# Metaformer block with position-aware row attention and a sigmoid recurrence: projections and relative parts as four 32x32 matmuls, relative parts by image pairs, elementwise work dealt anew to ScalarE and GpSimd

## The chip, the cores and the metric

One core of one Trainium2 chip runs the kernel. The metric is the device time of one execution in microseconds; the time before is the median of three runs. All data is float32.

## The reference, cut to what matters

The input x has 16 images of 32 x 32 x 32 (channel, row, position). The block normalises over the last axis, attends, adds the input, normalises again, multiplies by a 32x32 matrix, normalises over the batch, and runs a recurrence.

```python
x = x + attention(layernorm(x, 1e-6))         # below
t = tokens(x); n = layernorm(t, 1e-5)
q, k, v = Wq @ y, Wk @ y, Wv @ y              # over channels, per (row i, position j)
qk  = sum_i q[n,c,i,j] * k[n,c,h,j] / d       # per position j: scores between rows i and h
qrq = sum_i q[n,c,i,j] * rq[c,h,i] / d        # relative parts, linear in y
krk = sum_i k[n,c,i,j] * rk[c,h,i] / d
w   = softmax(qk + Gq*qrq + Gk*krk, axis=3)
out = w . (Gv1*v)  +  w . (Gv2*rv)            # weighted sum, and relative values
wx  = n @ W.T ; wx = batchnorm(wx)*gamma + beta
y_t = sigmoid(wx_t + y_{t-1} @ V.T)           # 1024 steps per image in the token order
out = t + y
```

In the kernel q and k are never formed alone: u = (Wk.T Wq / d) y is projected, and the scores are u against y. The relative parts come from one factor r, made out of Wq, Wk, rq, rk and the gates, applied to y.

## The kernel before, in words

**Layout.** 128 partitions hold 4 groups (g) of 32 channels, that is 4 images; the free dimension holds 4 image quarters (q, "images" below), 32 rows and 32 positions, so that one q is 1024 columns. A half or unit is 16 rows (512 columns, one PSUM bank). Engines run in a hand-written order, and named semaphores tie them together.

**First normalisation** (lines 595 to 638 on VectorE, 341 to 346 on GpSimd, 414 to 441 on ScalarE). Per part: sum over the last axis (`ln_mean`), mean by a `tensor_scalar` (L601), centring (`ln_minus`, L158; on VectorE for the two halves of image 0, on GpSimd for images 1 to 3), square on ScalarE (L419), sum of squares (L608), variance by a `tensor_scalar` (L611), square root on ScalarE (L437), reciprocal (L617) and scaling (L164).

**Weights.** SyncE loads everything, in the order of lines 278 to 296. GpSimd clears the block-diagonal tiles `w_bd`, `m_bd`, `r_tile` and `rv_bd` (L328 to L347). ScalarE writes the 32x32 diagonal blocks of `m_bd` (L431), of `r_bd` (`set_r`, L402, four copies of 32 x 1024) and of `rv_bd` (`set_rv`, L411, four more). VectorE spreads the gates (L565), turns the weights (L582) and writes `w_bd` (L587, L589).

**Attention on TensorE** (lines 877 to 1063). `project_u(q)` (L901) is two 128x128 matmuls of 512 columns; `scores(q, jh)` (L912) is 16 positions x 4 groups of 32x32 matmuls; `relative_scores` (L953) is, for all four images at once, 32 matmuls of 128x128 against 128 columns, one for each row; `project_values` (L943) is one 128x128 matmul a unit; `relative_values` (L931) spreads rv; `value_rows(b)` (L994) is four 128x128 matmuls; `weighted_sums(q, jh)` (L981) is 64 matmuls of 32x32; `project_wx(k)` (L1010) is one 128x128 matmul. Each float32 matmul stands in the profile as two LDWEIGHTS and two MATMUL rows. `keep_warm` (L887) issues matmuls whose result is not used. Long and short work are interleaved: `scores(2, 0)`, two value projections, `scores(2, 1)`, and so on; `value_rows` stands between halves of `weighted_sums`.

**Softmax.** VectorE adds scores and relative part out of PSUM (L650) and takes the row maximum (L655); GpSimd subtracts it (L354); ScalarE takes exp (L461); VectorE sums (L659), inverts (L661) and multiplies (`weights`, L663). `turn_values` (L643) transposes the values, reading them with a stride. 

**Second normalisation and wx.** VectorE adds the relative values and the input (`add_relative`, L680), then the weighted sum (`residual`, L689), sum and mean (L694, L696), sum of squares and variance (L705, L708), reciprocal (L713), transpose (`t_turn`, L727) and the batch statistics (L732). GpSimd centres (L361) and scales (L367) units 0 to 6, ScalarE squares (L484), takes roots (L489) and copies wx out of PSUM (L494). The last unit is centred and scaled on VectorE (L699, L717). `bn_aggr` (L789) ends this stage.

**Recurrence** (L1084 on TensorE, L546 on ScalarE, L810 on VectorE) and the output (L317, L323, L302) follow.

## Time and profile before

| | |
|---|---|
| time of the kernel, median of 3 runs | 159.18 us (157.61 to 159.52) |
| span of the profiled execution | 157.0 us |
| the runs' time less that span | 0.6 to 2.5 us, 2.2 at the median |
| busy: TensorE matmul, VectorE, ScalarE, GpSimd | 116.0, 121.8, 66.5, 48.1 us |
| attention and normalisations, to the end of L789 | 0 to 126.0 us |
| recurrence and output | 126.0 to 157.0 us |

The span goes from the first to the last instruction of one execution; a run's time holds what lies around it as well. In the profile PE is TensorE's matmuls, PEld its weight loads, DVE VectorE, ACT ScalarE, POOL GpSimd and SP SyncE. In a timeline row stand start, duration, engine, line, operation, what is written and read, and the number of instructions that were merged; in brackets stands the idle time of the engine before it and what ended it, where "issue" means that nothing in the profile accounts for it.

### The profile page before, as it was taken

The numbers are of one execution on the slowest core, as the hardware profiler recorded it, in microseconds if no ns is written. First come the engines' busy times: TensorE is split into PE (matmuls) and PEld (weight loads), VectorE is DVE, ScalarE is ACT, GpSimd is POOL, SyncE is SP. The second block draws the span as 40 slices with busy tenths as digits, with TensorE's granted clock in tenths as the row PEclk, the third lists the DMA queues.
The fourth block names the chain that finished last, engine by engine and source line by source line (L and its number), as shares of the span: only waits on it lengthen the run. The fifth ranks groups of instructions, "written<-read, shape, count | busy, mean of one in ns | idle before, by whom it ended". The sixth has DMA issues, their size and how long they took to land.

```text
span 157.0 us, 5384 instructions
## 1 busy us (share of the span) xinstructions
PE 116.0 (74%) x2404; PEld 80.3 (51%) x2404; DVE 121.8 (78%) x190; ACT 66.5 (42%) x155; POOL 48.1 (31%) x48
## 2 busy tenths in 40 slices
PE   0856969049996999858889955995795679999500
PEld 0412364027995563843559955651541147999500
DVE  1988999984044919859894888979999959788993
ACT  3431665054662440951410052134313447999600
POOL 6911935900004403104000222754532000002950
PEclk9996895857999599755999996598699955999955
DMA  3692000000000000000000000000000000000467
GB/s 138 172 301 47 0 4 4 0 0 0 0 8 4 0 8 4 4 4 0 4 4 4 4 0 4 4 4 0 4 0 2 0 4 2 0 0 0 138 183 218
DMA packets 6611, 5.02 MB, mean 32 GB/s; under 512 B 1756, under 2 KB 5852, under 8 KB 6588
## 3 DMA queue, kind: packets, MB, share of 16 engines
q1 hardware_dynamic: 6588, 4.67, 10.5%
q8 instruction: 19, 0.31, 0.8%
q14 instruction: 4, 0.03, 0.1%
HBM read 2.58 MB, written 2.10 MB: 30 GB/s over the span
## 4 chain that ended last, share of the span: by engine, by line
DVE 43%; PE 31%; ACT 14%; issue 6%; POOL 2%; DMA 2%; ACTq 0%
PE ps L912 8%; ACT warm L546 5%; PE ps L953 5%; DVE stat L611 4%; PE ps L901 4%; PE ps L943 4%; DVE xin L317 3%; DVE stat L694 3%; DVE stat L599 3%; DVE x L689 3%; DVE stat L601 3%; DVE stat L705 3%; DVE u_tile L727 3%; DVE y L323 3%; PE ps L994 3%
## 5 line engine op out<-in xcount | busy, mean ns | idle before, releaser
L981 PE MATMUL ps<-att,yt_tile 32*32 32x32 f32 x1024 | 16.6, 229 | 5.6 <-issue 3.9
L901 PE MATMUL ps<-y,m_bd 128*128 128x512 f32 x16 | 13.6, 1000 | 9.3 <-ACT u_tile L395 6.1
L981 PEld LDWEIGHTS ps<-att,yt_tile 32*32 32x32 f32 x1024 | 15.3, 129 | 9.5 <-issue 8.5
L912 PEld LDWEIGHTS ps<-y,u_tile 32*32 32x32 f32 x1024 | 15.6, 145 | 8.5 <-issue 8.4
L912 PE MATMUL ps<-y,u_tile 32*32 32x32 f32 x1024 | 16.7, 228 | 4.1 <-issue 4.1
L354 POOL TENSOR_TENSOR att<-att,soft 128x1024 f32<-128x1024 f32 x4 | 7.7, 1916 | 33.6 <-DVE soft L655 33.6
L650 DVE TENSOR_TENSOR att<-ps,bias_tile 128x1024 f32<-128x1024 f32 x4 | 4.9, 1224 | 16.0 <-ACT bias_tile L451 8.1
L484 ACT ACTIVATE square<-x2n 128x512 f32<-128x512 f32 x8 | 5.0, 628 | 24.9 <-POOL x2n L361 24.4
L887 PE MATMUL ps<-xin 128*128 128x512 f32 x22 | 14.8, 824 | 0.0
L323 POOL TENSOR_TENSOR y<-xin,x 128x256 f32<-128x256 f32 (+1 forms) x7 | 7.1, 1046 | 24.7 <-DVE xin L317 24.7
L1010 PE MATMUL ps<-u_tile,w_bd 128*128 128x512 f32 x16 | 10.5, 751 | 4.8 <-DVE u_tile L727 4.2
L361 POOL TENSOR_TENSOR x2n<-x,stat 128x512 f32<-128x512 f32 x7 | 7.3, 1048 | 21.8 <-DVE stat L696 21.7
L810 DVE TENSOR_SCALAR ps<-bias_tile,bnv 128x512 f32<-128x512 f32 (+1 forms) x18 | 12.4, 762 | 1.9 <-ACT warm L546 1.8
L901 PEld LDWEIGHTS ps<-y,m_bd 128*128 128x128 f32 x16 | 4.3, 299 | 15.4 <-issue 15.3
L367 POOL TENSOR_TENSOR x2n<-x2n,stat 128x512 f32<-128x512 f32 x7 | 7.3, 1048 | 11.0 <-DVE stat L713 11.0
L1084 PEld LDWEIGHTS ps<-warm,w_bd 128*128 128x128 f32 x80 | 10.0, 205 | 1.0 <-DVE ps L810 0.5
L1084 PE MATMUL ps<-warm,w_bd 128*128 128x128 f32 x80 | 9.9, 289 | 0.0
L943 PE MATMUL ps<-y,w_bd 128*128 128x512 f32 x16 | 9.4, 716 | 0.0
L887 PEld LDWEIGHTS ps<-xin 128*128 128x128 f32 x22 | 5.5, 267 | 6.8 <-issue 5.8
L546 ACT ACTIVATE warm<-ps 128x128 f32<-128x128 f32 x40 | 8.9, 276 | 0.2
L456 ACT COPY r_tile<-ps 128x512 f32<-128x512 f32 x8 | 4.7, 584 | 9.0 <-PE ps L943 9.0
L994 PE MATMUL ps<-att,rv_bd 128*128 128x128 f32 x64 | 7.9, 280 | 0.7 <-DVE att L663 0.7
(97 smaller groups left out, 227.2 us busy)
## 6 DMA issues: line engine op xcount, KB each, us to landing
out_dram<-y SPq DMA_DIRECT2D x8, 256.0 KB, 2.4
xin<-in_x_dram SPq DMA_DIRECT2D x3, 512.0 KB, 6.3
xin<-in_x_dram SPq DMA_DIRECT2D x2, 256.0 KB, 2.8
r_in<-in_L_conv_rq_dram SPq DMA_DIRECT2D x1, 128.0 KB, 4.8
r_in<-in_L_conv_rk_dram SPq DMA_DIRECT2D x1, 128.0 KB, 5.7
rv_in<-in_L_conv_rv_dram SPq DMA_DIRECT2D x1, 128.0 KB, 7.4
gates<-in_L_conv_Gv_dram SPq DMA_DIRECT2D x2, 0.5 KB, 4.9
wsmall<-in_L_conv_Wk_dram SPq DMA_DIRECT2D x1, 16.0 KB
```

Source lines behind the costliest of these rows:

```text
L323: return eng.tensor_tensor(result[:, :, rows, :], back[:, at:at + P * k].rearrange("p (q i j) -> p q i j", q=Q, i=k), x2[:, :, rows, :], A ...
L546: nc.scalar.activation(state_out(t, r), rec_slot(t, r).rearrange("p (q c) -> p q c", q=Q), ACT.Sigmoid).then_inc(S["state"], 1)
L810: return nc.vector.tensor_scalar(out, rows, scl, shift, ALU.mult, ALU.add)
L887: ins = nc.tensor.matmul(bank(k), xin[:, 0, 0:4, :].rearrange("p i j -> p (i j)"), xin[:, 0, 0:16, :].rearrange("p i j -> p (i j)"), start ...
L901: nc.tensor.matmul(bank(k), m_bd[:, :], y[:, q, 16 * k:16 * (k + 1), :].rearrange("p i j -> p (i j)"), start=True, stop=True).then_inc(S[" ...
L912: ins = nc.tensor.matmul(ps[p, half_scores(q, j // 16), C * (j % 16):C * (j % 16 + 1)], u[p, q, :, j], y[p, q, :, j], start=True, stop=True)
L943: nc.tensor.matmul(bank(k % 2), w_bd[:, 0, :], unit(y, k).rearrange("p i j -> p (i j)"), start=True, stop=True).then_inc(S["value_product" ...
L953: ins = nc.tensor.matmul(bank(6 + b % 2)[:, P * k:P * (k + 1)], r_bd[:, ROWS * b + k, :], y[:, :, ROWS * b + k, :], start=True, stop=True)
L981: ins = nc.tensor.matmul(ps[p, WSUM_BANK[q] + jh, C * (j % 16):C * (j % 16 + 1)], v_t[p, q, j, :], att[p, q, :, j], start=True, stop=True)
L994: ins = nc.tensor.matmul(rows[:, :, k, :], rv_bd[:, ROWS * b + k, :], att[:, :, ROWS * b + k, :], start=(k == 0), stop=True, skip_group_ch ...
L1010: nc.tensor.matmul(bank(WX_BANK[k % 2]), w_bd[:, 1, :], tokens[:, 16 * (k % 2):16 * (k % 2 + 1), k // 2, :], start=True, stop=True).then_i ...
L1084: nc.tensor.matmul(rec_slot(t, r), w_bd[:, 2, :], state_in(t, r), start=False, stop=True, skip_group_check=True).then_inc(S["preact"], 1)
```

## The change

- `m_bd`, `r_bd`, `rv_bd` and the value part of `w_bd` go. `m_fac`, `r_fac`, `rv_t` and `wv` hold the factor once for each group of 32 partitions, and each 128x128 matmul that used them becomes four 32x32 matmuls, one a group. `w_bd` keeps two block-diagonal matrices (W and V).
- The relative scores and the relative values are made for two images at a time, in four parts of eight rows, each row being four matmuls of 32x32 against 64 columns.
- ScalarE copies the relative values out of PSUM into `x2`, and GpSimd adds the input (`add_input`); VectorE's `add_relative` goes. GpSimd multiplies by the softmax's reciprocal (`weigh`) and centres all parts of the first normalisation; it also writes `w_bd`.
- The variance's scale and epsilon go into ScalarE's square root. The means are made by `scalar_tensor_tensor` with a tile of zeros in place of `tensor_scalar`.
- ScalarE issues six of the DMAs (Wk, Wq, rq, rk, Gq, Gk), SyncE issues all of x first, rv is loaded four times, and ScalarE spreads the gates. `preload_act_table(ACT.Sqrt)` stands ahead of ScalarE's work.
- `values` is stored position-major, so that its transposition reads contiguously. TensorE's order is coarser.

```diff
-            for k in range(2):
-                    nc.tensor.matmul(bank(k), m_bd[:, :], y[:, q, 16 * k:16 * (k + 1), :].rearrange("p i j -> p (i j)"),
-                                     start=True, stop=True).then_inc(S["u_product"], 1)
+                for k in range(2):
+                    for g in range(G):
+                        p = group(g)
+                        ins = nc.tensor.matmul(bank(k)[p, :], m_fac[p, :],
+                                               y[p, q, 16 * k:16 * (k + 1), :].rearrange("p i j -> p (i j)"),
+                                               start=True, stop=True)
+                    ins.then_inc(S["u_product"], 1)
...
+            def eight_rows(n, by, of, done):
+                pair, part = n // PARTS, n % PARTS
+                for k in range(EIGHT):
+                    i = EIGHT * part + k
+                    for g in range(G):
+                        p = group(g)
+                        ins = nc.tensor.matmul(eight_bank(n)[p, 2 * C * k:2 * C * (k + 1)].rearrange("p (q j) -> p q j", q=2),
+                                               by[p, i, :], of[p, 2 * pair:2 * pair + 2, i, :], start=True, stop=True)
+                ins.then_inc(S[done], 1)
...
+            pe.wait_ge(S["x_in0"], 16)
+            keep_warm(2, 2)
+            relative_factor()
+            pe.wait_ge(S["m_set"], 1)
+            project_u(0)
+            scores(0)
+            project_u(1)
+            relative_scores(0)
+            scores(1)
+            project_u(2)
+            project_u(3)
+            relative_scores(1)
+            scores(2)
+            project_values(0)
+            project_values(1)
+            scores(3)
+            project_values(2)
+            project_values(3)
+            weighted_sums(0)
+            relative_values(0)
+            weighted_sums(1)
+            pe.wait_ge(S["x2_ready"], 2)
+            for n in (4, 5, 6, 7):
+                project_values(n)
+            weighted_sums(2)
+            project_wx(0)
+            project_wx(1)
+            relative_values(1)
+            project_wx(2)
+            weighted_sums(3)
+            project_wx(3)
...
+            mark_bank(6)
+            mark_bank(7)
+            mark_bank(0)
+            mark_bank(1)
+            project_wx(4)
+            mark_bank(4)
+            mark_bank(5)
+            project_wx(5)
+            project_wx(6)
+            project_wx(7)
```

VectorE's and GpSimd's new pieces, and VectorE's order:

```diff
+                nc.vector.scalar_tensor_tensor(out=stat[:, 1, q, rows], in0=stat[:, 0, q, rows], scalar=1.0 / C,
+                                               in1=nought[:, 0:k], op0=ALU.mult, op1=ALU.add).then_inc(S["ln_mean"], 1)
...
+            def add_input(n):
+                pool.wait_ge(S["relv_ready"], n + 1)
+                nc.gpsimd.tensor_tensor(eight(x2, n), eight(x2, n), eight(xin, n), ALU.add).then_inc(S["x2_part"], 1)
...
+            score_max(0)
+            score_max(1)
+            weight_sum(0)
+            dve.wait_ge(S["rv_scaled"], 1)
+            nc.vector.transpose(rv_t[:, :, :], rv_s[:, :, :]).then_inc(S["rv_set"], 1)
+            weight_sum(1)
+            score_max(2)
+            score_max(3)
+            weight_sum(2)
+            turn_values(0)
+            turn_values(1)
+            weight_sum(3)
...
+            residual(4)
+            residual(5)
+            bn_part(2)
+            bn_part(3)
+            t_sum2(4)
+            t_rstd(4)
+            t_sum2(5)
             t_rstd(5)
             t_turn(4)
-            bn_part(3)
             residual(6)
             residual(7)
+            t_turn(5)
+            t_sum2(6)
             t_rstd(6)
+            t_sum2(7)
+            bn_part(4)
             t_turn(6)
             t_rstd(7)
             t_turn(7)
```

ScalarE's start:

```diff
+            load_small(3, Wk, "wqk_in")
+            load_small(4, Wq, "wqk_in")
+            for k, a in enumerate((rq, rk)):
+                act.dma_start(r_in[group(k), :], a.rearrange("c h i -> c (h i)")).then_inc(S["r_in_s"], 16)
+            load_gate(0, Gq, "gates_in")
+            load_gate(1, Gk, "gates_in")
+            nc.scalar.preload_act_table(ACT.Sqrt)
...
+            spread_out(0, 4)
+            spread_out(1, 3)
+            act.wait_ge(S["m_product"], 1)
+            nc.scalar.mul(m_fac[:, :], ps[:, 1, 0:C], 1.0 / d).then_inc(S["m_set"], 1)
+            ln_square(0)
+            ln_square(1)
```

## Rows read from the trace of the kernel before

**Rows 1.** The page's part 1: busy us (share of the span) xinstructions.
```profile
PE 116.0 (74%) x2404; PEld 80.3 (51%) x2404; DVE 121.8 (78%) x190; ACT 66.5 (42%) x155; POOL 48.1 (31%) x48
```
**Rows 2.** Timeline of TensorE's matmuls through the dense 32x32 work.
```profile
18.77 3.05 PE L912 MATMUL ps<-y,u_tile 32*32 32x32 f32 x200
23.16 1.03 PE L912 MATMUL ps<-y,u_tile 32*32 32x32 f32 x56 [1.34 <-issue]
...
44.54 3.84 PE L912 MATMUL ps<-y,u_tile 32*32 32x32 f32 x255
49.67 0.25 PE L912 MATMUL ps<-y,u_tile 32*32 32x32 f32 x1 [1.29 <-issue]
...
62.66 3.61 PE L912 MATMUL ps<-y,u_tile 32*32 32x32 f32 x234
67.73 0.51 PE L912 MATMUL ps<-y,u_tile 32*32 32x32 f32 x19 [1.47 <-issue]
...
71.28 0.54 PE L981 MATMUL ps<-att,yt_tile 32*32 32x32 f32 x23 [1.51 <-issue]
...
110.49 2.02 PE L981 MATMUL ps<-att,yt_tile 32*32 32x32 f32 x128
```
**Rows 3.** Waits, whole span: us in total, times, longest.
```profile
PE ps L912 <- issue: 4.1, 3, 1.5
PE ps L981 <- issue: 3.9, 3, 1.7
```
**Rows 4.** The page's part 3, the queue that brings instructions.
```profile
q8 instruction: 19, 0.31, 0.8%
```
**Rows 5.** Timeline, matmuls of 512 columns against 128x128 weights.
```profile
54.62 1.98 PE L943 MATMUL ps<-y,w_bd 128*128 128x512 f32 x4
...
71.75 4.28 PE L943 MATMUL ps<-y,w_bd 128*128 128x512 f32 x6
```
**Rows 6.** Windows: length, PE, PEld, DVE, ACT, POOL busy (x), PEclk, DMA share, GB/s.
```profile
52.70:53.70 1.00, 1.00 (x73) 1.00 (x76) 0.97 (x2) 0.59 (x1) 1.00 (x1) 0.50 0.00 0
108.87:125.99 17.12, 12.28 (x148) 5.06 (x147) 16.09 (x34) 5.48 (x13) 5.24 (x5) 0.90 0.01 1
```
**Rows 7.** Timeline and the page's part 6: when y of image 0 is ready; a gate's DMA.
```profile
12.46 0.69 DVE L164 TENSOR_TENSOR y<-y,stat 128x512 f32<-128x512 f32 x1
...
gates<-in_L_conv_Gv_dram SPq DMA_DIRECT2D x2, 0.5 KB, 4.9
```
**Rows 8.** Groups by line, shapes apart, whole span: busy us, mean ns of one.
```profile
L663 DVE TENSOR_TENSOR att<-att,soft 128x1024 f32<-128x1024 f32 x4 | 5.2, 1302 | 0.1
L680 DVE TENSOR_TENSOR x<-ps,xin 128x512 f32<-128x512 f32 x8 | 5.1, 675 | 2.3 <-PE ps L994 2.3
L643 DVE STREAM_TRANSPOSE yt_tile<-r_tile 128x1024 f32<-128x1024 f32 x4 | 7.8, 1950 | 0.5 <-ACT r_tile L456 0.5
L727 DVE STREAM_TRANSPOSE u_tile<-x2n 128x512 f32<-128x512 f32 x8 | 5.3, 687 | 0.0
L655 DVE TENSOR_REDUCE soft<-att 128x32 f32<-128x1024 f32 x4 | 4.9, 1220 | 0.1
L354 POOL TENSOR_TENSOR att<-att,soft 128x1024 f32<-128x1024 f32 x4 | 7.7, 1916 | 33.6 <-DVE soft L655 33.6
L361 POOL TENSOR_TENSOR x2n<-x,stat 128x512 f32<-128x512 f32 x7 | 7.3, 1048 | 21.8 <-DVE stat L696 21.7
L456 ACT COPY r_tile<-ps 128x512 f32<-128x512 f32 x8 | 4.7, 584 | 9.0 <-PE ps L943 9.0
L411 ACT COPY rv_bd<-ps 32x1024 f32<-32x1024 f32 x4 | 4.0, 1006 | 5.6 <-PE ps L931 5.5
```
**Rows 9.** Timeline: VectorE's operations that met GpSimd's.
```profile
26.22 5.34 DVE L611 TENSOR_SCALAR stat<-stat 128x32 f32<-128x32 f32 x1
...
52.52 1.92 POOL L354 TENSOR_TENSOR att<-att,soft 128x1024 f32<-128x1024 f32 x1 [2.71 <-DVE soft L655]
...
53.98 1.53 DVE L663 TENSOR_TENSOR att<-att,soft 128x1024 f32<-128x1024 f32 x1
```

More of the change, by code:

```diff
@@ L177, in wx_rows, with eight, eight_bank, ln_scale @@
             return wx_q[:, 16 * (k % 2):16 * (k % 2 + 1), k // 2, :]
+        def eight(t, n):
+            pair, part = n // PARTS, n % PARTS
+            return t[:, 2 * pair:2 * pair + 2, EIGHT * part:EIGHT * (part + 1), :]
+        def eight_bank(n):
+            return bank(REL_BANK[n % 2])
+        def ln_scale(eng, n, done):
+            q, row, k = LN_PARTS[n]
+            eng.tensor_tensor(y[:, q, row:row + k, :], y[:, q, row:row + k, :],
+                              stat[:, 3, q, row:row + k].unsqueeze(2).broadcast_to([P, k, C]),
+                              ALU.mult).then_inc(S[done], 1)
         def round_row(t):
@@ new lines, in _ @@
+            u_half(2, 0)
+            u_half(2, 1)
+            u_half(3, 0)
+            u_half(3, 1)
+            score_exp(1)
+            for n in range(PARTS, 2 * PARTS):
+                rel_out(n)
+            score_exp(2)
+            value_out(0)
+            value_out(1)
+            value_out(2)
+            value_out(3)
+            score_exp(3)
+            relv_out(0)
+            relv_out(1)
+            relv_out(2)
+            relv_out(3)
+            for n in (4, 5, 6, 7):
+                value_out(n)
@@ new lines, in _ @@
+            ln_mean(1)
+            ln_mean(2)
+            ln_sum2(0)
+            ln_sum2(1)
+            ln_rstd(0)
+            ln_out(0)
+            ln_rstd(1)
+            ln_out(1)
+            ln_mean(3)
+            ln_sum2(2)
+            ln_rstd(2)
+            ln_out(2)
+            ln_mean(4)
+            dve.wait_ge(S["w_in"], 16 * 3)
+            nc.vector.transpose(wturned[:, :, :], wsmall[:, 0:3, :]).then_inc(S["turned"], 1)
+            ln_sum2(3)
+            ln_rstd(3)
+            ln_sum2(4)
@@ L778, in _ @@
             t_turn(7)
-            bn_part(4)
             dve.wait_ge(S["marked"], 2)
@@ L959, in _ @@
-            project_u(0)
-            relative_factor()
-            scores(0, 0)
-            scores(0, 1)
-            project_u(1)
-            project_u(2)
-            wait_y(pe, Q - 1)
-            relative_scores()
-            def weighted_sums(q, jh):
+                for jh in range(2):
+                    for j in range(16 * jh, 16 * (jh + 1)):
+                        for g in range(G):
+                            p = group(g)
+                            ins = nc.tensor.matmul(ps[p, SCORE_BANK[q] + jh, C * (j % 16):C * (j % 16 + 1)],
+                                                   u[p, q, :, j], y[p, q, :, j], start=True, stop=True)
+                    ins.then_inc(S["score_product"], 1)
@@ L970, in weighted_sums, with relative_values @@
+            def relative_values(pair):
+                pe.wait_ge(S["weights"], 2 * pair + 2)
+                pe.wait_ge(S["rv_set"], 1)
+                pe.wait_ge(S["rel_ready"], 2 * PARTS)
+                for n in range(PARTS * pair, PARTS * (pair + 1)):
+                    if n >= 2:
+                        pe.wait_ge(S["relv_ready"], n - 1)
+                    eight_rows(n, rv_t, att, "relv_product")
+            def weighted_sums(q):
                 pe.wait_ge(S["weights"], q + 1)
@@ L998, in mark_bank @@
-            def mark_bank(k):
-                pe.wait_ge(S["x2_ready"], UNITS - 2 if k >= 6 else UNITS)
-                keep_warm(k, 1).then_inc(S["marked"], 1)
+                    pe.wait_ge(S["score_sum"], 4)
+                for jh in range(2):
+                    for j in range(16 * jh, 16 * (jh + 1)):
+                        for g in range(G):
+                            p = group(g)
+                            ins = nc.tensor.matmul(ps[p, WSUM_BANK[q] + jh, C * (j % 16):C * (j % 16 + 1)],
+                                                   v_t[p, q, j, :], att[p, q, :, j], start=True, stop=True)
+                    ins.then_inc(S["wsum_product"], 1)
```

602 lines of the change are left out of this document (250 added, 352 removed).

## The prediction

> **What bounds the kernel now.** I read the page's busy shares first, then TensorE's timeline, its waits, the DMA queues, and last the windows and the groups by line. The busy shares name two engines: VectorE 121.8 us and TensorE 116.0 us of 157.0 [rows 1]. Most of the edit takes work from VectorE, so the question is what TensorE allows once VectorE is quicker.
>
> In TensorE's timeline the reader is to see holes inside runs of 32x32 matmuls. `scores(0)` does 200 MATMUL rows in 3.05 us, stands still for 1.34 us and does the other 56; more holes of 1.29, 1.47 and 1.51 us follow [rows 2]. The waits put six such holes, 8.0 us, down to "issue": no engine released them [rows 3]. From the first hole to the second lie 56 + 8 (L901) + 64 (L953) + 255 = 383 MATMUL rows, or three times 128; from the third to the fourth about 127. 
>
> The Trainium skill, "Runtime: NRT & Kernel Launch", section "Instruction fetch mechanics", also has 16 KiB blocks of 256 instructions, but says that crossing one is mostly hidden. The size agrees with rows 3 and 4, the "mostly hidden" does not. By the page there would be no growing cost here; that is the first rival.
>
> **The change, part by part.**
>
> *TensorE's instruction count.* Relative scores and relative values go from 64 MATMUL rows each to 2 pairs x 4 parts x 8 rows x 4 groups x 2 = 512 each; the projections of u and of values from 16 each to 64 each. That is +992, from 2404 to about 3390: nearly eight more packets, all in the stage that ends at 126.0.
>
> *What a projection costs.* Four 32x32 matmuls of 512 columns do as much as the block diagonal if they run side by side, and save nothing. A pair of full-width matmuls took 0.99 us (1.98 for two halves) and 1.43 (4.28 for three) [rows 5]; I take 1.15 for a half. Do four groups run side by side? With the granted clock at 0.50 (1.2 GHz) 73 MATMUL rows of 32 columns started in 1 us [rows 6], 14 ns each. 512 columns take at least the 0.71 us of rows 5's slower row (4.28 / 6) at that clock, so 32 columns take 45 ns or more: 45/14 says that over three are under way at once, of four that could be. Bounds for 512 columns: 0.99 us a half, and, if a group's second pass held up the next group's first, five passes instead of two, 2.5 to 3.6 us. I take side by side, as rows 6 stand nearest.
>
> *What VectorE loses.* `weights` 5.2 us, `add_relative` 5.1 us, four strided transpositions of 1.95 us that read contiguously now (between 1.95 and 2 x 0.69 = 1.37; I take 1.37) [rows 8], the variances, and the stalls of `tensor_scalar` behind GpSimd, of which one lasted 5.34 us [rows 9]. ScalarE loses eight block copies of 1.0 us and gains eight of 0.58; GpSimd gains four of 1.92 and eight of 1.05 [rows 8]. Both have room [rows 1], but their steps now lie in chains.
>
> *The `scalar_tensor_tensor`.* It reads two tiles of SBUF. A two-tile operation meeting GpSimd's subtraction took 1.53 us against a mean of 1.30 [rows 9, 8]; GpSimd's ended at 54.44, and 1.22 us of work after 54.3 is just what VectorE shows. So the mean can still wait, up to 1.9 us, and only the long train is avoided. I charge 0.8 us near the end and nothing ahead of it, where TensorE's packets cover it. The Trainium skill, "SBUF — State Buffer", section "Who interferes with whom", says the same against this edit: a VectorE instruction with two SBUF inputs contends with a GpSimd instruction that reads SBUF.
>
> **The sum,** along TensorE:
>
> 1. Start. ScalarE now issues six DMAs and waits for the gates ahead of its first square. A gate's DMA took 4.9 us to land [rows 7]; issued sixth, near 3.3 us, it lands near 8 by that row, and between 6 and 11 if half or one and a half times that is allowed. I take 8, so y of image 0 is ready near 12.6 us (before: 12.46 + 0.69 = 13.15 [rows 7]), and since the relative factor is already made, `scores(0)` starts at 16.0 instead of 18.77 [rows 2].
> 2. To the end of `scores(3)`: 4 x 256 score rows and 2 x 256 relative rows are 12 packets, 12 x 3.4 = 40.8. Eight projection halves add 9.2. They hide about 3.5 holes of 1.45, 5.1. End: 60.9. Before it was 67.73 + 0.51 = 68.24 [rows 2]. The change leads by 7.3 us.
> 3. `weighted_sums(0)` needs the turned values, which in VectorE's order stand behind the sum and maximum of image 3 and the sum of image 2: 3 x 1.22 + 0.35 + 1.37 = 5.4. Start: 66.3, before 68.0. Lead 1.7.
> 4. To the end of `weighted_sums(3)`: 4 x 256 + 2 x 256 rows, again 40.8; seven halves (four values, three of wx) 8.0; 4.5 holes hidden, -6.5; 2.5 for hand-offs from ScalarE and GpSimd, an estimate. End 111.1, before 110.49 + 2.02 = 112.5 [rows 2]. Lead 1.4.
> 5. The tail. In the 17.1 us after `residual(5)` VectorE was busy for 16.1 [rows 6]. The change keeps that list, less one `bn_part` that went ahead (0.7) and four variances (1.5 with their stalls): 14.9. But `residual(5)` is later against TensorE (last relative part, ScalarE's copy, GpSimd's addition), and `bn_part(3)` waits for `project_wx(3)`, now behind all of `weighted_sums(3)`: 1.15 + 0.6 + 0.1 after it. So 14.2 us of list remain from there, with 2 us of waits inside and the 0.8 above: 111.1 + 1.9 + 14.2 + 2.8 = 130.0, before 126.0.
>
> The recurrence and the output are untouched. That is +4.0 on the profiled execution: 161 us of span, and with the 2.2 us that lie around it at the median, 163.2. I put the time at **163 us**. VectorE becomes the idler engine, and TensorE pays for it in packets.
>
> **The rivals.**
>
> *A: the holes stay hidden; faster.* If a packet is ready as soon as it is needed, steps 2 and 4 lose eight and a half and seven and a half holes of 1.45, 23 us, of which VectorE's own order gives back about 6: 163 - 17 = 146. For it: VectorE has some 20 us less to do, and all six holes lie in dense runs, none where 32x32 work is mixed with 128-wide work. Against it: the change mixes less, and its runs are longer. With the holes at 1.0 us instead of 1.45 the time is 163 - 16 x 0.45 = 156, which is where faster by over 2% begins.
>
> *B: the four groups run one after another at 512 columns.* Sixteen halves at 2.5 us or more instead of 1.15 are +22 to +27, of which hidden holes give some back: about 183. The rule that speaks for it: the Trainium skill, "TensorE: Matmul & The Clock Gate", Part 3, has matmuls start and end in program order, and each group's two passes stand side by side in that order. Against it are the 14 ns of rows 6.
>
> *C: no difference.* The same chain with a packet ready after 3.2 us instead of 3.4 and half of the tail's waits: 24 x 0.2 + 1 = -6 at most, halved by what overlaps: 159 to 160.
>
> *D: the edit doesn't do what it says.* The `scalar_tensor_tensor` stalls as the `tensor_scalar` did, thirteen times, a few on the path: +3, 166. And if the sparse 32x32 work lowers the granted clock to 1.2 GHz for most of the stage, fifteen halves cost 0.5 more: +5, 168. These lie inside the forecast's upper end.
>
> **How the numbers follow.** Forecast with D: 0.50, slower by over 2% but for its lowest part. C 0.27, A 0.18, B 0.05. Two per cent, 3.2 us, is about what a measurement tells from no change. Faster by over 2%: 0.18; within: 0.28; slower: 0.54. The range reaches down to A with two thirds of a hole (153) and up to D with a late gate and a second slow term (174); beyond lie the whole of A and B.
>
> **What would show it.** Right: the instruction queue shows 26 or 27 packets; TensorE's idle time by "issue" grows from 8 to 20 us and more; `scores(3)` ends near 61, `weighted_sums(3)` near 111, `bn_aggr` near 130; VectorE is busy for under 100 us; a projection half of four groups lasts 1 to 1.4 us. Wrong: "issue" stays under 12 us and `weighted_sums(3)` ends before 100 (A); halves of 2.5 us (B); or the holes are as told, but another engine is late at each of them.

## The result, and the profile after

The changed kernel takes 182.5 us (180.54 to 185.12, 4 runs) against 158.84 us (157.61 to 159.52, 4 runs) beside it: a ratio of 1.146, 95% interval 1.137 to 1.154. It is slower by 23.7 us. (Medians are of all runs, and ratios of those alone that lie within 1.5% of their kernel's fastest, so 182.5 / 158.84 isn't exactly 1.146.) Forecast were 163, with 174 as the upper end. The direction was right, and the size was far off.

The profile's page of the changed kernel, parts 1 and 3, answers to [rows 1] and [rows 4]:

```profile
span 180.1 us, 7348 instructions
PE 120.9 (67%) x3390; PEld 79.4 (44%) x3390; DVE 93.1 (52%) x152; ACT 65.8 (37%) x156; POOL 61.3 (34%) x66
q8 instruction: 26, 0.43, 1.0%
```

VectorE lost 28.7 us of work, and the instructions come in 26 packets instead of 19, both as forecast. No engine is busier than TensorE's 67%. The waits of the changed kernel (total, times, longest) answer to [rows 3]:

```profile
PE ps L969 <- issue: 10.6, 7, 1.9
PE ps L908 <- issue: 9.4, 6, 2.0
PE ps L918 <- issue: 4.0, 5, 1.7
```

In these 18 holes TensorE stands still for 24.0 us with no engine to name for it; before it was 8.0 us in six. The timeline of its matmuls, against [rows 2]:

```profile
17.55 1.92 PE L895 MATMUL ps<-y,m_fac 32*32 32x512 f32 x16 [0.95 <-DVE y L156]
20.17 2.93 PE L908 MATMUL ps<-y,u_tile 32*32 32x32 f32 x190 [0.70 <-ACT u_tile L437]
24.18 1.14 PE L908 MATMUL ps<-y,u_tile 32*32 32x32 f32 x65 [1.09 <-issue]
...
36.18 2.03 PE L908 MATMUL ps<-y,u_tile 32*32 32x32 f32 x128 [2.01 <-issue]
39.91 1.41 PE L908 MATMUL ps<-y,u_tile 32*32 32x32 f32 x82 [1.70 <-issue]
...
67.36 0.33 PE L908 MATMUL ps<-y,u_tile 32*32 32x32 f32 x7 [1.25 <-issue]
67.49 3.63 PE L940 MATMUL ps<-y,wv 32*32 32x512 f32 x16
72.94 1.69 PE L969 MATMUL ps<-att,yt_tile 32*32 32x32 f32 x104 [1.81 <-DVE yt_tile L653]
76.55 2.02 PE L969 MATMUL ps<-att,yt_tile 32*32 32x32 f32 x128 [1.93 <-issue]
80.28 0.55 PE L969 MATMUL ps<-att,yt_tile 32*32 32x32 f32 x24 [1.71 <-issue]
...
95.74 7.10 PE L940 MATMUL ps<-y,wv 32*32 32x512 f32 x32
...
126.86 1.19 PE L969 MATMUL ps<-att,yt_tile 32*32 32x32 f32 x69 [1.73 <-issue]
```

In the dense stretches the merged counts show the packets themselves: runs of exactly 128 matmuls, a hole, then the rest. From the start of one such run to the start after the next hole is 3.73 us (36.18 to 39.91, and 76.55 to 80.28). Line by line against before:

| event | before | after | forecast |
|---|---|---|---|
| scores(0) starts | 18.77 | 20.17 | 16.0 |
| scores(3) ends | 68.24 | 67.7 | 60.9 |
| weighted_sums(0) starts | 68.0 | 72.94 | 66.3 |
| weighted_sums(3) ends | 112.5 | 128.05 | 111.1 |
| bn_aggr ends | 126.0 | 149.2 | 130.0 |

What lies behind bn_aggr is the same in both (31.0 and 30.9 us). So the miss of 19.2 us has four parts: 4.2 at the start, 2.6 in the first dense phase, 10.3 in the second, 2.2 in the tail, less 0.2 between the phases.

### The profile page after: what moved, and what is told of

Read it like the earlier page. It is cut to its first block, busy times and chain, and to the rows that moved or that the text cites. A ratio compares the mean times of both kernels' runs of the same rounds, so it can differ in the third digit from the quotient of the medians.

```text
span 180.1 us, 7348 instructions
## 1 busy us (share of the span) xinstructions
PE 120.9 (67%) x3390; PEld 79.4 (44%) x3390; DVE 93.1 (52%) x152; ACT 65.8 (37%) x156; POOL 61.3 (34%) x66
## 4 chain that ended last, share of the span: by engine, by line
PE 44%; DVE 21%; issue 16%; ACT 11%; DMA 5%; ACTq 2%
PE ps L908 9%; PE ps L918 8%; PE ps L969 7%; PE ps L895 6%; PE ps L940 6%; PE ps L980 5%; DMA gates<-in_L_conv_Gk_dram 5%; ACT warm L585 4%; DVE xin L286 3%; DVE y L292 2%; PE ps L875 2%; DVE stat L706 2%; DVE u_tile L724 2%; ACT yt_tile L585 2%; DVE stat L694 2%
## 5 line engine op out<-in xcount | busy, mean ns | idle before, releaser
L969 PE MATMUL ps<-att,yt_tile 32*32 32x32 f32 x1024 | 16.8, 229 | 13.2 <-issue 10.6
L689 DVE TENSOR_TENSOR x<-ps,x 128x512 f32<-128x512 f32 x8 | 5.4, 675 | 20.6 <-POOL x L356 20.6
L940 PE MATMUL ps<-y,wv 32*32 32x512 f32 x64 | 14.5, 1032 | 0.0
L356 POOL TENSOR_TENSOR x<-x,xin 128x512 f32<-128x512 f32 x8 | 10.0, 1265 | 13.1 <-ACT x L457 13.1
L309 POOL TENSOR_TENSOR y<-xin,stat 128x1024 f32<-128x1024 f32 (+1 forms) x5 | 7.8, 1566 | 15.2 <-DVE stat L610 15.2
L918 PE MATMUL ps<-att,rv_t 32*32 32x64 f32 x512 | 10.5, 247 | 3.3 <-issue 3.3
L918 PEld LDWEIGHTS ps<-att,rv_t 32*32 32x32 f32 x512 | 9.7, 128 | 5.2 <-issue 5.2
L895 PE MATMUL ps<-y,m_fac 32*32 32x512 f32 x64 | 11.3, 843 | 0.9 <-DVE y L156 0.9
L616 DVE TENSOR_REDUCE stat<-square 128x32 f32<-128x1024 f32 (+1 forms) x5 | 4.9, 994 | 11.4 <-ACT square L418 11.4
L452 ACT COPY values<-ps 128x512 f32<-128x512 f32 x8 | 4.6, 584 | 17.0 <-PE ps L940 17.0
L530 ACT COPY bias_tile<-ps 128x512 f32<-128x512 f32 x8 | 4.6, 584 | 15.9 <-PE ps L980 15.9
```

Source lines behind the costliest of these rows:

```text
L309: nc.gpsimd.tensor_tensor(y[:, q, row:row + k, :], xin[:, q, row:row + k, :], stat[:, 1, q, row:row + k].unsqueeze(2).broadcast_to([P, k, C]),
L356: nc.gpsimd.tensor_tensor(eight(x2, n), eight(x2, n), eight(xin, n), ALU.add).then_inc(S["x2_part"], 1)
L895: ins = nc.tensor.matmul(bank(k)[p, :], m_fac[p, :], y[p, q, 16 * k:16 * (k + 1), :].rearrange("p i j -> p (i j)"), start=True, stop=True)
L918: ins = nc.tensor.matmul(eight_bank(n)[p, 2 * C * k:2 * C * (k + 1)].rearrange("p (q j) -> p q j", q=2), by[p, i, :], of[p, 2 * pair:2 * p ...
L940: ins = nc.tensor.matmul(bank(k)[p, :].rearrange("p (j h) -> p j h", h=C), wv[p, :], y[p, q, :, 16 * k:16 * (k + 1)].rearrange("p h j -> p ...
L969: ins = nc.tensor.matmul(ps[p, WSUM_BANK[q] + jh, C * (j % 16):C * (j % 16 + 1)], v_t[p, q, j, :], att[p, q, :, j], start=True, stop=True)
```

## The experiments

Fourteen kernels ran; they are told in four groups. Their edits are shown shortened, with plain names for slices of tiles. Names that begin with a_ are the changed kernel with an edit, with b_ the kernel before with one. The kernel before took 158.4 to 159.1 us beside them (medians).

**1. Are the holes packets of instructions? (a_long, b_twice)**

a_long: the relative parts as one long matmul for each group and part. It applies one row's factor to all eight rows of a part, so it leaves the true relative parts out; it has 896 MATMUL rows fewer.

```diff
-for k in range(EIGHT):
-    for g in range(G):
-        matmul(eight_bank(n)[p, 2*C*k:2*C*(k+1)], by[p, i, :], of[p, 2*pair:2*pair+2, i, :])
+for g in range(G):
+    matmul(eight_bank(n)[p, :], by[p, EIGHT*part, :], of[p, 2*pair:2*pair+2, EIGHT*part:EIGHT*(part+1), :])
```

> The changed kernel with each part of the relative scores and values made by one matmul of 512 columns a group instead of eight rows of 64 columns. The columns that pass through the array, the banks and all waits stay; the MATMUL rows go from 1024 to 128 in the two relative products. It leaves out seven of eight row factors, so it computes other relative parts. Theory (instruction packets of 128 matmul pairs, 3.4 to 3.9 us each in dense work): 7 packets fewer, 19 instead of 26; the 16 parts cost some 1.2 us each instead of half a packet of 3.8; the time falls from 182.5 by 14 to 22 us, to 161 to 168. Rival (the array's work and the order bound TensorE, not the fetching): 16 parts stay near 1.0 to 1.2 us each, the time stays within 3 us of 182.5.

Measured: 165.74 us (163.42 to 168.06, 2 runs), 19 packets. Its waits:

```profile
PE ps L969 <- issue: 5.1, 4, 1.7
PE ps L908 <- issue: 3.5, 4, 1.2
```

b_twice: the kernel before, with scores(1) issued twice, so that the matmuls of image 1 are done again with the same result.

```diff
-ins = nc.tensor.matmul(...)
+for _ in range(2 if q == 1 else 1):
+    ins = nc.tensor.matmul(...)
```

> The kernel before with each matmul of scores(1) issued twice, the same operands and the same result: 256 more MATMUL rows, two packets. Theory (packets): scores(1) costs two more packets at 3.4 to 3.9 us less what was hidden, +6 to +8 us: 165 to 167, and 21 packets. Rival (issue at 15 ns a pair alone): +3.8 us: 163.

Measured: 167.4 us, ratio 1.061 (1.048 to 1.074), 21 packets. The timeline of TensorE where the work was doubled:

```profile
50.92 2.13 PE L913 MATMUL ps<-y,u_tile 32*32 32x32 f32 x128 [1.24 <-issue]
54.37 2.15 PE L913 MATMUL ps<-y,u_tile 32*32 32x32 f32 x128 [1.32 <-issue]
57.83 0.27 PE L913 MATMUL ps<-y,u_tile 32*32 32x32 f32 x1 [1.30 <-issue]
```

256 more matmuls of 15 to 17 ns are about 4 us of work and cost 8.5. One hole stands after every 128, in this dense stretch; the rival's 3.8 falls. And 896 matmuls taken out of the changed kernel give 16.8 us back, with the same columns through the array; its holes fell from 24.0 to 8.6 us.

The traces also say when each packet comes. The DMA view of b_twice from 52 to 53 us (forty slices of 0.025 us; a transfer is put in the slice in which it starts, and the share is of 16 engines):

```profile
DMA  9000000000000000000000000000000000000000
q8 instruction: 1, 0.02, 6.0%
```

and that of the changed kernel from 37 to 38 us:

```profile
DMA  0000000000090000000000000000000000000000
q8 instruction: 1, 0.02, 8.0%
```

In b_twice the packet starts at 52.0, 1.1 us after the run of 128 at 50.92 began; its transfer takes 0.96 us (6.0% of 16 us), and the next run begins at 54.37, 1.4 us after it landed. That makes the 3.45 us from run to run. In the changed kernel it starts at 37.3, 1.1 us after 36.18, takes 1.28 us, and the run at 39.91 begins 1.3 us after it landed: 3.73 us, longer by the slower transfer. Read in the same way, each of the changed kernel's 18 holes ends 1.2 to 1.5 us after an instruction packet has landed. In both cases, then, the next packet is fetched only once TensorE is inside the one before it, and work that is shorter than this round leaves a hole. Why the fetch doesn't start earlier no run here shows.

**2. Do four 32x32 matmuls of 512 columns run side by side? (b_four)**

```diff
-nc.tensor.matmul(bank(k), m_bd[:, :], y[:, q, 16*k:16*(k+1), :])
+for g in range(G):
+    ins = nc.tensor.matmul(bank(k)[p, :], m_bd[p, p], y[p, q, 16*k:16*(k+1), :])
```

> The kernel before with the projections of u and of the values as four 32x32 matmuls of 512 columns each, nothing else changed (the factors are read out of the diagonal blocks). Theory (the four groups run side by side; what counts is the instruction count): 96 more MATMUL rows, under one packet: 0 to +3 us, halves of 1.0 to 1.8 us as before. Rival (the groups run one after another): halves of 2.5 us or more and +15 to +25 us.

Measured: 158.72 us (10 runs), ratio 1.004 (0.998 to 1.010). Its timeline:

```profile
53.94 0.60 PE L949 MATMUL ps<-y,w_bd 32*32 32x512 f32 x1
...
54.04 1.90 PE L949 MATMUL ps<-y,w_bd 32*32 32x512 f32 x15
```

Sixteen MATMUL rows (two halves, four groups, two passes each) take 2.0 us, as the full-width pairs do in [rows 5]. Side by side is shown, and the forecast's rival B falls, although its 183 is the number that came out: right by accident, for a reason that isn't there. The changed kernel's own row at 17.55 says the same, 0.96 us a half. The rule quoted for B (matmuls start and end in program order) doesn't keep four row and column groups apart.

**3. The parts that could explain the miss (a_loads, a_values, b_contig, a_inter, a_mix, a_mix_long)**

a_loads: the six loads of ScalarE's queue go back to SyncE's, in the order of before.

```diff
+load_small(3, Wk) load_small(4, Wq) load_gate(0, Gq) load_gate(1, Gk)   # SyncE, after load_x(1)
+sp.dma_start(r_in ...) x2                                               # SyncE, after load_x(2)
-load_small(3, Wk) load_small(4, Wq) act.dma_start(r_in ...) x2 load_gate(0, Gq) load_gate(1, Gk)   # ScalarE
```

> The changed kernel with all loads back on SyncE's queue, the small ones between the halves of x and its rest, as before the change. Theory (the start is late because the gates and Wk, Wq wait behind 2 MB of x): scores(0) starts near 16 us instead of 20.2, and since TensorE is fetch-bound behind it, all of 3 to 5 us comes through to the end: 178 to 180. Rival (VectorE's and GpSimd's order sets the start or makes up for it): under 1.5 us of gain.

Measured: 178.12 us, ratio 1.129 (1.117 to 1.142): 4.4 us better. The intervals of the two ratios overlap a little, but the slowest of its five runs (178.73) is below the fastest of the changed kernel (180.54). ScalarE's timeline, the changed kernel first:

```profile
12.62 0.83 ACT L431 ACTIVATE spread<-wsmall,gates 32x128 f32<-32x128 f32 x2 [6.43 <-DMA gates<-in_L_conv_Gk_dram]
```

and the same instruction in a_loads:

```profile
6.31 0.83 ACT L434 ACTIVATE spread<-wsmall,gates 32x128 f32<-32x128 f32 x2 [4.29 <-DMA gates<-in_L_conv_Gk_dram]
```

A gate of a few bytes, issued near 4 us on a queue of its own, landed at 12.6, while issued on SyncE ahead of image 1 it was there at 6.3. scores(0) starts at 17.8 in a_loads instead of 20.2. Queue and order changed together here, so which of the two counts isn't separated.

b_contig: in the kernel before, value projections that read y with a stride of 32 elements, so that the transposition reads contiguously.

```diff
-matmul(bank(k % 2), w_bd[:, 0, :], unit(y, k))
+matmul(bank(k % 2) as (j h), w_bd[:, 0, :], y[:, k // 2, :, 16*(k % 2):16*(k % 2 + 1)] as (j h))
-transpose(v_t[:, q], values[:, q] as (j h))
+transpose(v_t[:, q], values[:, q])
```

> The kernel before with the values stored position-major, so that the value projection reads y with a stride and the transposition on VectorE reads contiguously. Theory: the transpositions take 1.2 us instead of 1.95 and two or three of them lie on the chain ahead of the weighted sums: -1 to -2.5 us. Rival (VectorE isn't what TensorE waits for there, the packets are): within 1 us of before; or the strided read slows the projections: slower.

Measured: 162.09 us, ratio 1.026 (1.018 to 1.034). Its timeline and a window on it:

```profile
55.80 3.69 PE L943 MATMUL ps<-y,w_bd 128*128 128x512 f32 x4
```

```profile
55.80:59.40 3.60, 3.60 (x9) 0.71 (x4) 1.63 (x2) 1.64 (x2) 0.59 (x1) 1.00 0.03 7
```

The transposition fell from 1.95 to 1.24 us. But four MATMUL rows take 3.69 us at the full granted clock, where [rows 5] has 1.98 for the same four: a moving operand with a stride of 128 bytes costs 0.92 us for 512 columns instead of 0.50. I had charged nothing for it. The expectation's last rival, a slower projection, holds.

a_values undoes just that in the changed kernel.

> The changed kernel with its values kept channel-major again, as before the change: the four 32x32 matmuls of a value half read 512 neighbouring columns instead of a stride of 32 elements, and VectorE's transposition reads with the stride (1.95 us instead of 1.22, four of them). The number of TensorE's instructions stays. Theory (the strided moving operand is one of the terms missing from the sum): the 64 matmuls of L940 fall from a mean of 1032 ns to about 600 ns, a half from 1.72 us to about 1.0 to 1.2, the eight halves together by 4 to 5 us, of which the four ahead of weighted_sums(0) are partly covered; transpositions give 0.7 back twice on the path: time 180 +- 1. Rival (the value projections cover packets that arrive anyway, so they cost nothing): 182.5 or up to 1.5 more, and idle time by 'issue' grows by what the projections lose.

Measured: 182.8 us (181.49 to 185.56, 4 runs): no difference from 182.5. The mean of L940 fell from 1032 to 830 ns:

```profile
62.62 3.64 PE L940 MATMUL ps<-y,wv 32*32 32x512 f32 x14
...
72.29 1.92 PE L940 MATMUL ps<-y,wv 32*32 32x512 f32 x16
78.41 1.70 PE L969 MATMUL ps<-att,yt_tile 32*32 32x32 f32 x104 [4.21 <-DVE yt_tile L653]
...
100.67 5.48 PE L940 MATMUL ps<-y,wv 32*32 32x512 f32 x32
```

The gain is there in places. The two halves ahead of weighted_sums(0) fell from 3.63 to 1.92 us, but the wait for VectorE behind them grew from 1.81 to 4.21; the four later halves fell from 7.10 to 5.48, and the whole phase from 55.1 to 53.1. The two halves at 62.62 did not change at all (3.64, as the two from 58.54 to 61.97 in the changed kernel, of which the windows are shown further down): in both, the granted clock stood at 0.50 there, which is 1.2 GHz. At that level the strided read costs nothing beside it; at 2.4 GHz it takes the gain of the clock away. My expectation of 180 missed, and the rival's number (182.5 to 184) holds, though not for its reason: idle time by "issue" stayed at 23.9 us. The eight halves gave up 3 to 4 us of TensorE's time, and the longer wait for VectorE and a later start took it. (The profiled execution was the slowest of the four, 185.56 us, and its gates landed late, so I compare its phases and not its end.)

a_inter deals the long matmuls between halves of scores(1) to (3) and weighted_sums(1), to hide more holes.

```diff
-scores(1); project_u(2); project_u(3)
+scores(1, (0,)); project_u(2); scores(1, (1,)); project_u(3)
-scores(2); project_values(0); project_values(1); scores(3); project_values(2); project_values(3)
+scores(2, (0,)); project_values(0); project_values(1); scores(2, (1,)); scores(3, (0,)); project_values(2); project_values(3); scores(3, (1,))
-weighted_sums(1); project_values(4); project_values(5)
+weighted_sums(1, (0,)); project_values(4); project_values(5); weighted_sums(1, (1,))
```

> The changed kernel with its long matmuls dealt between the halves of scores and of weighted_sums(1): project_u(2) and (3) between and behind the halves of scores(1), project_values(0) to (3) between the halves of scores(2) and (3), project_values(4), (5) between the halves of weighted_sums(1). Same instructions, another order on TensorE. Packet theory: each long matmul group among 32x32 work hides up to 1 to 1.9 us of a hole; three or four more holes are hidden, idle time by 'issue' falls from 24 to 19 us and the time to 176 to 180. Rival (a packet's arrival sets the pace and long work already hides all it can): 182.5 +- 1.5.

Measured: 180.06 us (177.63 to 181.98), ratio 1.126 (1.113 to 1.139), against 1.146 for the changed kernel. The intervals touch and the runs overlap, so a gain of some 2 us is likely and not shown. Of its 20.5 us of "issue", 5.2 are one wait of the kind told under a_mix.

a_mix has a_loads, a_values and a_inter together.

> The changed kernel with three repairs together: all loads on SyncE in the order of before (178.1 alone), values channel-major again, long matmuls dealt between halves. If the three are terms of one sum along TensorE: 178 minus 2 minus 3 to 4, that is 172 to 174. If they hide the same holes and give back one another's gain: 176 to 178. Either way it stays well above the kernel before, since TensorE still has 26 packets instead of 19: under 163 would speak against the packets as the main term.

Measured: 176.42 us (175.31 to 177.21), ratio 1.110 (1.100 to 1.119). One by one the three gave 4.4, -0.3 and 2.4 us, 6.5 in all; together they gave 6.1. Within the spread of the runs they add up. The expectation's second case has the right number, but what fell short of 172 to 174 is the size of the parts and not their sum. TensorE's timeline, then VectorE's:

```profile
75.82 3.50 PE L972 MATMUL ps<-att,yt_tile 32*32 32x32 f32 x231 [5.93 <-issue]
```

```profile
69.96 1.22 DVE L661 TENSOR_TENSOR att<-ps,bias_tile 128x1024 f32<-128x1024 f32 x1 [9.20 <-PE ps L911]
71.21 1.22 DVE L666 TENSOR_REDUCE soft<-att 128x32 f32<-128x1024 f32 x1
72.35 1.21 DVE L670 TENSOR_REDUCE soft<-att 128x32 f32<-128x1024 f32 x1
73.59 0.35 DVE L672 RECIPROCAL soft<-soft 128x32 f32<-128x32 f32 x1
73.86 3.65 DVE L656 STREAM_TRANSPOSE yt_tile<-values 128x1024 f32<-128x1024 f32 x2
```

The bracket says "issue" for 5.93 us, but this is no packet: the last one landed 4.8 us before the run began. It is the chain of step 3 on VectorE: sum, maximum, sum, reciprocal, and the first of two transpositions (73.86 + 1.9) ends 0.06 us ahead of weighted_sums(0). When project_values(2) and (3) moved ahead of the second half of scores(3), nothing was left to cover the chain. A label of a wait has to be held against the other engines' timelines before it is added up: of a_mix's 24.2 us of "issue", 18.3 are holes.

a_mix_long is a_mix with a_long's relative parts, so it too leaves the true relative parts out.

> The changed kernel with the loads in the order of before, values channel-major, long matmuls dealt between halves (176.4 with these), and the relative parts by one 32x32 matmul of 512 columns for each group and part, which multiplies all eight rows of a part by one row's factor (so other relative parts are computed, with 896 fewer MATMUL rows). Theory of packets: back to 19 packets, 16 to 18 less than 176.4: 158 to 161; with the fold of the variances still in it, it should even come under the kernel before (158.7) if nothing else were lost. Rival (the repairs and the packets hide one another): 163 to 166, as the relative parts alone gave 165.7.

Measured: 164.81 us, ratio 1.042 (1.024 to 1.059). That is a_long's 165.74 again, within its spread: once 896 matmuls are gone, the three repairs are worth nothing that shows. scores(0) starts 2.4 us earlier than in a_long (17.86 against 20.26), but weighted_sums(0) starts 1.8 us later (67.39 against 65.58), after 5.96 us of idle time for VectorE's chain, as above. The rival's number holds; that this wait alone decides the end is argued and not shown.

**4. What the good parts are worth (b_fold, b_fold_stt, b_pool, b_fsp, a_unfold)**

b_fold: the kernel before, with the variance folded into ScalarE's square root.

```diff
-nc.vector.tensor_scalar(var, sum2, 1.0 / C, EPS, ALU.mult, ALU.add)
-nc.scalar.activation(std, var, ACT.Sqrt)
+nc.scalar.activation(std, sum2, ACT.Sqrt, bias=eps, scale=1.0 / C)
```

> The kernel before with one part of the change alone: the variances' scale and epsilon go into ScalarE's square root, so VectorE's thirteen small tensor_scalar operations of the variances go, the 5.34 us one among them. Theory (that part of the change is good where TensorE isn't the bound): y of image 3 is ready 4 to 5 us earlier, TensorE's 6.1 us idle ahead of project_u(2) shrinks, and each t chain loses 0.2 us: 153 to 156. Rival (other waits take its place, since the image 2 scaling and two memsets still run on GpSimd): within 1 us of before.

Measured: 149.5 us, ratio 0.942 (0.933 to 0.950), more than expected. y of image 3 is ready at 27.7 us instead of 33.5: the variance of [rows 9] that took 5.34 us from 26.22 ended with GpSimd's memsets of `rv_bd` and `warm` (27.04 to 31.53), and it is gone. TensorE's 6.14 us of idle time ahead of project_u(2), which ended at 33.61, is gone too, and weighted_sums(3) ends at 102.94 instead of 112.5.

b_fold_stt: also the means by scalar_tensor_tensor with a tile of zeros.

> As the kernel with the variances folded into the square root, and the means by scalar_tensor_tensor with a tile of zeros, as the change has them. Theory (two inputs from SBUF wait for GpSimd only where it reads): the mean behind the r_tile memset loses its 2.3 us stall, the means behind GpSimd's centring keep theirs: 1 to 2.5 us less than with the fold alone. Rival (it stalls just as tensor_scalar does): no difference, or +0.5 us from its longer duration.

Measured: 147.71 us (144.93 to 149.04), bn_aggr ends at 114.9 where b_fold has 116.3. The runs of the two versions overlap by a little (b_fold 148.80 to 153.24), so this step rests on the rows more than on the medians. The groups by line, b_fold first:

```profile
L608 DVE TENSOR_SCALAR stat<-stat 128x16 f32<-128x16 f32 x2 | 3.4, 1704 | 0.1
L608 DVE TENSOR_SCALAR stat<-stat 128x32 f32<-128x32 f32 x3 | 1.9, 642 | 0.1
```

and b_fold_stt:

```profile
L611 DVE SCALAR_TENSOR_TENSOR stat<-stat,nought 128x16 f32<-128x16 f32 x2 | 0.4, 214 | 0.1
L611 DVE SCALAR_TENSOR_TENSOR stat<-stat,nought 128x32 f32<-128x32 f32 x3 | 1.9, 650 | 0.1
```

One of the two of 16 elements meets GpSimd's 3.51 us memset of `r_tile`, which reads nothing. Its row in the timeline of b_fold, and then in that of b_fold_stt:

```profile
5.70 3.14 DVE L608 TENSOR_SCALAR stat<-stat 128x16 f32<-128x16 f32 x1
```

```profile
5.74 0.17 DVE L611 SCALAR_TENSOR_TENSOR stat<-stat,nought 128x16 f32<-128x16 f32 x1
```

The three of 32 elements stand beside GpSimd's subtractions, which read SBUF: 642 and 650 ns, no difference. The Trainium skill, "SBUF — State Buffer", section "Who interferes with whom", has a VectorE instruction with two SBUF inputs contend with a GpSimd instruction that reads SBUF, and not with one that only writes it; the trace agrees with both halves. The stall behind the memset of `rv_bd` only moved on, in both versions: 3.50 us of VectorE's `spread_v`, a tensor_scalar, stand there now.

b_pool: the multiplication by softmax's reciprocal goes to GpSimd.

```diff
-nc.vector.tensor_tensor(att[:, q], att[:, q], soft_recip, ALU.mult)
+nc.gpsimd.tensor_tensor(att[:, q], att[:, q], soft_recip, ALU.mult)   # one image later in GpSimd's order
```

> The kernel before with the multiplication by the softmax's reciprocal on GpSimd, behind its subtraction for the next image, as in the change. Theory (moving work off VectorE is worth nothing where its step is in a chain): the multiplication takes 1.9 instead of 1.25 us and waits for its turn, VectorE gains 5 us of room: -1 to +2 us. Rival (VectorE's busy time is what counts): -3 to -5 us.

Measured: 159.21 us, ratio 1.002 (0.997 to 1.007). Five us of VectorE's work gone, and the time stays.

b_fsp is b_fold_stt with b_pool's edit.

> The kernel before with the variance folded into ScalarE's square root, the means by scalar_tensor_tensor (these two together gave 147.7) and, new, the multiplication by softmax's reciprocal on GpSimd, where it alone gave nothing. VectorE loses 5 us of work, the instruction count of TensorE stays 19 packets. Theory (with the head start of TensorE gone, VectorE's list of sums, maxima and transpositions behind scores(3) is late again): 145 to 147. Rival (the time between is set by TensorE's packets, as before): 147.7 +- 1.

Measured: 147.58 us (145.29 to 147.92). The same as b_fold_stt; VectorE's load doesn't bound that version either.

a_unfold: the changed kernel with its variances and means as tensor_scalars again.

> The changed kernel with one part of the edit undone: the variances are thirteen tensor_scalars on VectorE again (in place) and the means are tensor_scalars again. TensorE's program is the changed kernel's. In the kernel before, the same two edits were worth 11 us (158.4 to 147.7). Theory (the changed kernel had that gain, and the packets and the cold clock took about 35 us, not 23): undoing it costs 8 to 12, time 191 to 195. Rival (in the changed kernel TensorE's packets set the pace, so the gain never showed): 182.5 to 185, with scores(0) later by what the start loses and scores(3), weighted_sums(3) at the same times as before.

Measured: 185.98 us (181.93 to 186.67, 4 runs). Three of the four lie near 186 and one at 181.93, inside the changed kernel's own range (180.54 to 185.12), so no loss is shown; the medians differ by 3.5 us at most. The theory's 8 to 12 falls. In its profiled execution (185.97) scores(0) starts 1.3 us later, but 0.9 of that is a later landing of the gates (13.52 against 12.62), which the edit doesn't touch.

The rival's number fits, its reason isn't needed. The groups of the variances by line, in the kernel before and in a_unfold:

```profile
L611 DVE TENSOR_SCALAR stat<-stat 128x32 f32<-128x32 f32 x3 | 6.4, 2133 | 0.1
```

```profile
L615 DVE TENSOR_SCALAR stat<-stat 128x32 f32<-128x32 f32 x3 | 1.8, 588 | 0.1
```

The same tensor_scalars that stalled for 5.34 and 3.14 us in the kernel before and in b_fold stall for less than 1 us here. They had stood behind the 3.51 us memsets of `rv_bd` and `r_tile`, and these memsets went with the block diagonals. In the changed kernel there was no such train left to get away from.

## Why the prediction was wrong

**The reading of the trace was right.** 26 packets, holes inside dense 32x32 work, "issue" above 20 us, VectorE under 100 us, four groups side by side: all as foretold, and the packets' timing in group 1 bears the reading out. Of the signs, the length of a projection half (1 to 1.4 us) and the three moments (61, 111 and 130) failed. The Trainium skill, "Runtime: NRT & Kernel Launch", section "Instruction fetch mechanics", says a crossing of such a block is mostly hidden; here 8 us of holes became 24, so the measurement decides against it for dense 32x32 work. Rival A (146 to 156) fell with b_twice, B with b_four, C with the result. What failed is the sizes in the sum along TensorE: the landing of the gates, the price of a projection half, the holes and 64-column matmuls of step 4, and the waits of the tail.

**Step 1, the start (4.2 of the 19.2 us).** "I take 8" for the gates was the failing term; they landed at 12.6, above my upper bound of 11. I scaled one row of a transfer's time [rows 7] and did not ask what shares the DMA engines: the profile's page shows 149 and 319 GB/s in the first two of its forty slices. That this traffic is what delayed the gates is likely and not shown. a_loads shows the price of the new order, 2.4 us of start and 4.4 in all.

**Steps 2 and 4, the projections (7.2 us).** I took 1.15 us a half from [rows 5], two fast cases. Measured in the first phase: eight halves in 12.3 us (3.3 + 5.6 + 3.4), not 9.2; in the second 12.1 (7.10 + 3.84 + 1.12), not 8.0. Windows of the changed kernel, with the granted clock in the third column from the end:

```profile
25.20:28.40 3.20, 3.20 (x26) 0.86 (x21) 0.17 (x1) 0.59 (x1) 2.79 (x5) 0.50 0.02 5
41.20:46.70 5.50, 5.50 (x44) 1.65 (x37) 5.03 (x5) 1.76 (x3) 2.73 (x2) 0.61 0.00 1
58.70:61.90 3.20, 3.20 (x25) 0.84 (x17) 2.44 (x2) 0.00 (x0) 0.46 (x1) 0.50 0.02 5
95.97:102.85 6.88, 6.87 (x32) 1.10 (x24) 1.25 (x1) 1.76 (x3) 0.00 (x0) 0.70 0.01 2
```

Before each of these stretches TensorE had done 32x32 work with holes in it, and the projections then ran at 1.2 GHz in whole or part: 1.4 to 1.9 us a half but for the last, against 0.96 at 17.55 at full clock. For the most part that is rival D's term, 0.5 a half, which I had only let into the upper end; the fifteen halves cost 7.2 us more than charged, 0.48 a half. Some 1.6 us of the 7.2 are another term, at which I had put nothing: the strided read, since the four later value halves took 7.10 us here and 5.48 in a_values. The trace of before had the warning too: its project_u rows of line L901, not among those that I took, run at a clock of 0.58 and need about 1.67 a half.

**Step 4, the rest of the second phase (6.1 us).** Holes: 17.4 less 6.5 hidden is 10.9; measured are 13.9 us in ten holes. A dense packet of 128 pairs took 3.46 to 3.73 us from start to start, not 3.4; [rows 2] showed four holes, of 1.3 to 1.5, and the two others of [rows 3] were 0.7 and 1.7. I had no row of a long dense stretch. The 32- and 64-column work: twelve packets at 1.95 are 23.4; 26.5 were measured (55.1 less holes, projections and 2.65 of waits for engines, where 2.5 was estimated). The difference is in the relative values: 64 columns at a low clock need more than the 15 ns of a 32-column matmul:

```profile
80.63:83.36 2.73, 2.73 (x119) 2.57 (x110) 0.00 (x0) 0.59 (x1) 0.10 (x1) 0.57 0.02 6
84.38:86.38 2.00, 2.00 (x128) 1.84 (x128) 0.00 (x0) 1.09 (x2) 0.88 (x2) 1.00 0.03 8
```

At the full clock 128 of them fit in 2.00 us; at 0.57, 103 take 2.73. "128 pairs at 15 ns" had used the 32-column rate for both. In the first phase the holes came out 2.2 us below the sum and the rest 1.7 above, which is why it missed by 2.6 only.

**Step 3 was right.** 5.4 us from the end of scores(3) to weighted_sums(0) were forecast, 5.2 measured, and it was the chain that I had named: 67.74 to 72.87 on VectorE, with the transposition at 1.22 instead of 1.37 us.

**Step 5, the tail (2.2 us).** 18.9 was forecast from the end of weighted_sums(3) to bn_aggr, and 21.15 measured. VectorE's list came out (14.2 forecast, 14.39 busy), but partly by luck: 16.1 less 0.7 and less 1.5 is 13.9 and not the 14.9 from which I went on. The waits were 6.8 us and not 4.7: of these 2.7 before the first instruction (1.9 forecast), because project_wx(3) was slow too, and 1.55 for a ScalarE copy ahead of the last one. One scalar_tensor_tensor waited, 0.81 us, as charged.

**Where the expected gain went.** The fold and the zeros tile are worth 11 us in the kernel before, where they take VectorE out from behind two long memsets; the changed kernel has no such memsets, and nothing of these 11 us is shown to be left in it (a_unfold). b_pool shows that 5 us less of VectorE's work are worth nothing in the kernel before; the move of `add_relative` wasn't tried by itself. Against that stand the 992 additional matmuls, of which 896 cost 16.8 us (a_long), and the load order (4.4). The strided read costs 3.7 us in the kernel before (b_contig) and nothing that shows in the whole time of the changed one (a_values). I had kept the direction by the packets alone and priced the colder clock as a tail risk. The three repairs gave 6.1 us together, and nothing once the packets had gone; a_long leaves 7 us over the kernel before. What these 7 us consist of wasn't settled.

**The version that beats both** is b_fold_stt, 147.71 us: 19% under the changed kernel and 7% under the one before, with the block diagonals kept.

## What to carry to other kernels

Count TensorE's instructions before trading one wide matmul for many small ones: where 32x32 work is dense, every 128 matmul pairs brought a hole of mostly 1.0 to 2.0 us, because a packet held only 2 us of work and the next was ready some 3.5 us after it was entered. The long matmuls behind such stretches ran at 1.2 GHz for whole or part. Price a moved matmul from rows at the clock that it will have, not from the fastest rows. And make the edits one at a time: two small ones that took VectorE out from behind memsets gave 11 us, while the large edit that holds them both lost 23.7.

## What the runs showed that I had not expected

- A moving operand read with a stride of 32 elements takes 0.92 us for 512 columns at 2.4 GHz, against 0.50 contiguous (b_contig); at 1.2 GHz two four-group halves take 3.64 us either way (a_values and the changed kernel). Why the clock was low just there wasn't tried.
- A packet's hole isn't constant: 1.0 to 2.2 us in the dense stretches of the changed kernel and a_unfold, at the same instruction pattern. In the two cases of group 1 it is mostly the length of the packet's own transfer that differs, 0.96 and 1.28 us; between 76.55 and 80.28 it is the start, 1.5 us into the run instead of 1.1.
- A small load on another engine's queue isn't early because it is small: 8 us from issue to use here, beside the large loads of another queue.
- scalar_tensor_tensor didn't wait for a memset on GpSimd (0.17 us) and waited for a subtraction there (0.88 us). The memset of `r_tile` held up a mean and that of `rv_bd` a variance, and with the variance gone it held up `spread_v` instead.
